# Layer 2 attention: the output step between the third and fourth score, and the maxima at set places

## The reference

```python
qkv = x @ w_qkv
q, k, v = jnp.split(qkv, 3, axis=-1)
q, k, v = (to_heads(q), to_heads(k), to_heads(v))
q = _apply_rope(q, cos, sin)
k = _apply_rope(k, cos, sin)
scores = jnp.einsum('bhqd,bhkd->bhqk', q, k) * scale
causal = jnp.tril(jnp.ones((S, S), dtype=bool))
scores = jnp.where(causal, scores, jnp.finfo(scores.dtype).min)
attn = jax.nn.softmax(scores, axis=-1)
out = jnp.einsum('bhqk,bhkd->bhqd', attn, v)
```

## Time and profile before

| | us |
|---|---|
| median of three executions | 1165.45 |
| lowest and highest | 1164.25, 1167.2 |
| the profiled execution | 1160.65 |
| its span, first to last instruction | 1159.4 |
| TensorE busy in the span | 921.2 (79%) |
| VectorE busy | 846.7 (73%) |
| ScalarE busy | 633.1 (55%) |
| GpSimd busy | 519.9 (45%) |
| layer 2's scores (L1974), first and last | 511.2 to 750.1 |
| layer 2's groups of maxima (L1919), first and last | 477.7 to 719.1 |

### The profile page before, as it was taken

How to read it: one execution, slowest core, us unless ns; L and a number is a source line. 1 busy time by engine, 2 the same in 40 slices (tenths; PEclk the granted TensorE clock), 3 DMA queues, 4 the chain that set the end, 5 groups by cost and what they waited for, 6 DMA issues and landing times. The chain is left out here.

```text
span 1159.4 us, 18534 instructions
## 1 busy us (share of the span) xinstructions
PE 921.2 (79%) x5579; PEld 562.6 (49%) x5579; DVE 846.7 (73%) x1648; ACT 633.1 (55%) x1370; POOL 519.9 (45%) x527
## 2 busy tenths in 40 slices
PE   5978799999667866568888888769999285778992
PEld 3423354444445552222223322258999154766981
DVE  7887999999999367878887887176544658986333
ACT  3487799897243443327766667834543293135432
POOL 2066798899501423301111111225653566326763
PEclk9978899999877988759999999959999587868996
DMA  9000000000000301410011110061110200001113
GB/s 318 1 1 1 1 1 1 1 1 1 1 1 0 146 1 34 131 29 23 22 27 18 30 29 3 2 256 38 45 37 27 76 0 1 1 28 47 52 47 123
DMA packets 28014, 46.29 MB, mean 40 GB/s; under 512 B 8720, under 2 KB 16408, under 8 KB 26896
## 3 DMA queue, kind: packets, MB, share of 16 engines
q1 hardware_dynamic: 22672, 34.66, 9.6%
q0 software_dynamic: 4096, 8.35, 2.5%
q10 hardware_dynamic: 1152, 2.10, 0.5%
HBM read 34.45 MB, written 12.58 MB: 41 GB/s over the span
## 5 line engine op out<-in xcount | busy, mean ns | idle before, releaser
L2106 DVE TENSOR_REDUCE sb_l_mxp<-ps 128x2 f32<-128x1024 f32 (+3 forms) x152 | 171.3, 1163 | 41.0 <-PE ps L1919 39.8
L1048 POOL TENSOR_TENSOR sb_gs<-sb_hs,sb_xp 128x512 f32<-128x512 f32 x128 | 162.4, 1304 | 23.9 <-PE ps L680 19.4
L2049 ACT ACTIVATE sb_l_pT<-ps 128x512 f32<-128x512 f32 (+3 forms) x256 | 111.4, 520 | 76.9 <-PE ps L1974 75.7
L680 PE MATMUL ps<-sb_gs,sb_ident 128*128 128x512 f32 x256 | 132.2, 608 | 0.2
L3058 PE MATMUL ps<-sb_hT,sb_f_shared 128*128 x936 | 118.5, 276 | 1.9 <-ACT sb_hT L3091 1.9
L3058 PEld LDWEIGHTS ps<-sb_hT,sb_f_shared 128*128 128x128 f32 x936 | 110.8, 192 | 3.1 <-issue 2.7
L1974 PE MATMUL ps<-sb_l_qk 51*128 51x512 bf16 (+3 forms) x384 | 88.4, 333 | 18.6 <-ACT sb_l_pT L2049 8.3
L3158 POOL DMA_INDIRECT moe_y<-sb_f_rows,sb_f_rowi x64 | 64.2, 1002 | 52.4 <-DVE sb_f_rows L3130 40.1
L3099 ACT ACTIVATE sb_f_hid<-ps 128x512 f32<-128x512 f32 x78 | 46.6, 597 | 73.9 <-PE ps L3058 73.9
L3069 PE MATMUL ps<-sb_sw_f_out,sb_f_hid 128*128 x624 | 82.7, 276 | 0.7 <-DVE sb_f_hid L3119 0.6
L951 ACT ACTIVATE sb_dA<-sb_dt,sb_negA 128x512 f32<-128x512 f32 x109 | 77.8, 713 | 9.7 <-DVE sb_hs L854 9.0
(11 more groups left out here) (418 smaller groups left out, 2139.6 us busy)
## 6 DMA issues: line engine op xcount, KB each, us to landing
sb_sw_f_in<-w_f_in SPq DMA_DIRECT2D x2, 2048.0 KB, 9.9
sb_sw_f_out<-w_f_out SPq DMA_DIRECT2D x2, 2048.0 KB, 12.7
sb_l_qk<-spill SPq DMA_DIRECT2D x112, 32.0 KB
spill<-sb_l_parts SPq DMA_DIRECT2D x12, 256.0 KB, 3.0
moe_y<-c_f_zero SPq DMA_DIRECT2D x1, 2048.0 KB, 9.2
sb_sw_f_up<-w_f_up SPq DMA_DIRECT2D x1, 2048.0 KB, 12.0
moe_h<-sb_f_rows SPq DMA_DIRECT2D x8, 256.0 KB, 4.4
sb_f_rows<-moe_y SPq DMA_DIRECT2D x8, 256.0 KB, 6.1
```

What stands on the lines that cost most here:

```text
L680: pe.matmul(ps[:, 4 + e * CPB + hf, :], ident[:], gs[:, p % SL, :], start=False, stop=n == DS - 1).then_inc(acc, 1)
L1048: gp.tensor_tensor(gs[:, q % SL, :], hs[:, q % SL, :], cs[:, k % 2, hf * CH:(hf + 1) * CH], ALU.mult).then_inc(times_c, 1)
L2049: ac.activation(pT[e % 3][:, h, 0:width], ps[:, bank[n_bank], 0:width], ACT.Exp, scale=L2_SCALE).then_inc(exped, 1)
L2106: dv.tensor_reduce(dst, src, AX_X, ALU.max).then_inc(max_out, 1)
```

## The change

Two edits in `order()`, and one step is split.

- **Output between scores.** If the output that is pending belongs to a block without a mask, it is issued behind the third score of the next block, not behind the fourth. If it belongs to a masked block it stays behind the fourth. So it moves in B1 to B4. To go with it, the copy moves from behind the second score to behind the first.
- **Set places for groups.** A flag `may` is true only behind an output of a masked block, behind a third score while such an output is pending, behind a fourth score when the output has already been issued, and at the start of a set. Only there may groups be taken, as many as the lead then asks for. In B1 to B4 all groups thus stand behind the fourth score, two at a time.
- **`largest` split from `rows`.** VectorE's reduction to the largest is a step of its own, one group earlier: behind the first group of the next set, before its second ("all").

```diff
@@ -1771,6 +1771,8 @@
                   ("heads", 7, 1, 0, 512, 0), ("heads", 7, 1, 0, 512, 1), ("heads", 7, 2, 512, 384, 0), ("heads", 7, 2, 512, 384, 1),
                   ("diagonals", 0, 7)]
 
+        is_diagonal = lambda qc, kt: kt * P >= qc * CH
+
         def lead(at):
 
             knots = [(0.0, LEAD), (NSET - 2.0, NSET - 2.0 + LEAD), (NSET - 1.25, NSET)]
@@ -1780,16 +1782,18 @@
             return NSET + 1
 
         def order():
-
+            at_gap = lambda step: step[0] == "pv" and is_diagonal(*step[2:4]) or step[0] == "score" and (
+                step[4] == 2 and bool(pending) and is_diagonal(*pending[0][2:4]) or step[4] == 3 and not pending)
 
             out_cost = sum((qc + 1) * CH - max(qc * CH, kt * P) + 100 for qc in range(CPB) for kt in range((qc + 1) * TPC)) * HG
 
             def maxima(s):
                 for i, group in enumerate(GROUPS):
                     yield ("max", s, group), s + (i + 1) / len(GROUPS)
-                    if s > 0 and i == 1:
-                        yield ("rows", s - 1), s + (i + 1) / len(GROUPS)
+                    if s > 0 and i < 2:
+                        yield (("largest", "rows")[i], s - 1), s + (i + 1) / len(GROUPS)
                 if s == NSET - 1:
+                    yield ("largest", s), s + 1
                     yield ("rows", s), s + 1
                 yield None, None
 
@@ -1805,7 +1809,9 @@
                         for h in range(HG):
                             done += width + 100
                             yield ("score", s, qc, kt, h, q0, width), s + done / out_cost
-                            if h == 1 and u > 0 and kt == 1:
+                            if h == 2 and pending and not is_diagonal(*pending[0][2:4]):
+                                yield pending.pop(), s + done / out_cost
+                            if h == 0 and u > 0 and kt == 1:
                                 yield ("copy", u - 1), s + done / out_cost
                             if h == 1 and u > 0 and kt == 2:
                                 yield ("back", u - 1), s + done / out_cost
@@ -1821,9 +1827,10 @@
                         (U // 2 + 1, 5): ("project", 1), (U - 1, 4): ("turn", 2), (U - 1, 6): ("project", 2)}
             pending = []
             at_max, at_out, s_max, s_out = 0.0, 0.0, 0, 0
+            may = True
             gen_max, gen_out = maxima(0), None
             while s_out < NSET:
-                if s_max < NSET and at_max < lead(at_out if gen_out else s_out):
+                if s_max < NSET and may and at_max < lead(at_out if gen_out else s_out):
                     step, at = next(gen_max)
                     if at is None:
                         s_max += 1
@@ -1838,9 +1845,11 @@
                 if at is None:
                     s_out += 1
                     gen_out = None
+                    may = True
                 else:
                     yield step
                     at_out = at
+                    may = at_gap(step)
             yield pending.pop()
             yield ("copy", CPB * NSET - 1)
             yield ("back", CPB * NSET - 1)
@@ -1886,7 +1895,6 @@
                 freed_by[bank[-1]] = (x_new, NCH * 4 + step[1] + 1)
         mixed_at = [CPB * (NSET // B * (c // CPB + 1) - 1) + c % CPB + 1 for c in range(NCH)]
         pv_bank = lambda u: spare_bank if u == U - 2 else 7
-        is_diagonal = lambda qc, kt: kt * P >= qc * CH
         pv_steps = [step for step in steps if step[0] == "pv"]
         masked_at = [sum(is_diagonal(qc, kt) for _, _, qc, kt, _ in pv_steps[:e + 1]) for e in range(len(pv_steps))]
 
@@ -2116,9 +2124,10 @@
                     reduce_group(n_max, s, step[2])
                     n_max += 1
                     max_done[s] = n_max
-                elif kind == "rows":
+                elif kind == "largest":
                     dv.wait_ge(max_out, max_done[s])
                     dv.tensor_reduce(mx[:, z, :], mxp[:, z].rearrange("p k h t -> p (h t) k"), AX_X, ALU.max).then_inc(mx_step, 1)
+                elif kind == "rows":
                     dv.wait_ge(max_mm, n_max + 1)
                     dv.tensor_scalar(mxT[:], ps[0:HG * TPB, n_max % 2 * 2, 0:P], -1.0, None, ALU.mult).then_inc(max_out, 1)
                     n_max += 1
```

## The result

The changed kernel took 1176.01 us (median of 4 runs, 1174.85 to 1180.28), beside 1165.48 us for the kernel before (4 runs): the ratio is 1.0105, 95% interval 1.0079 to 1.013. That is 10.5 us slower, where 10.1 were forecast. Compared a second time it was 1.0079 (1.0046 to 1.0113), 1173.25 against 1164.14 us. The profiled execution took 1174.85 us, with a span of 1173.6 us, and is 14.2 us longer than the profiled one of before.

A forecast was written before the change was run, and what follows sets the result against it. TensorE was taken as the bound, with the path of the maxima to the next first score nearly as long. Terms 9.0 + 1.3 + 0.3 - 0.5 = +10.1 us on 1165.45 gave 1175.5 us, range 1166 to 1182.

The forecast's parts named there:

- the sets with groups: Six sets (0 to 5) that hold the next set's groups of maxima: 1.5 us late each, 9.0 us together.
- the set of 31.3 to 31.8 us: Sign that the forecast is right: the time between first scores of successive sets would be 31.3 to 31.8 us.
- the faster rival: Removed waits pay and the maxima keep up: 1.63 us a set, 9.8 over six sets, giving 1155.7 us; chance 0.12.
- B1 and B3: Second and fourth key blocks, second query half: output waits about 1 us for the copy; diagonal group begins at 8.6 us.
- A1: Second key block of the first query half: the output waits for the copy, costing 0.2 us a set.
- The maxima: VectorE's last reductions begin at 9.6 us, pick-up at 13.5 instead of 11.8; next set's first score 1.4 us late.
- The first score waits for the transfers in every set: Sign that the forecast is right: each set's first score waits for the transfers of its maxima.
- TensorE's own row: Cross-check on TensorE alone: a diagonal group waits for a reduction; 1.2 us a set even if transfers were free.
- Set 6: Last diagonal group late by the output ahead, 1.00 us, plus 0.2 and 0.1 from two blocks: +1.3 us (0.5 to 1.8).
- Set 7: No groups; in four blocks the fourth score waits for the previous block's output, 0.1 us each: +0.3 (0 to 1.2).
- The start: Before the first score, moving the largest up removes VectorE's 0.49 us wait: -0.5 us (0 to -0.7).
- The clock rival: Longer pauses cost TensorE its upper clock once in each of seven sets: up to 1186 us, 1181 with half hidden; chance 0.08.

The follow-up runs named there:

- free places: The change without its set places, so groups of maxima may go wherever the ratio of work asks for one: 1167.7 us, ratio 1.0027.
- e_largest: The kernel before with only the largest moved, behind the first group of maxima: 1161.4 us, ratio 0.9962.
- e_places: The change with every output behind the fourth score of its block, as before, and the set places kept: 1164.0 us, ratio 0.9995.

## Why the prediction was right, and where its terms were off

The sum, +10.1 us, met +10.5 (and +9.1 the second time). The mechanism held, but that the number did is partly luck: the sets with groups were put 2.0 us too high, and a fall of the clock in set 7, left to a rival, gave 1.8 us back. Of the signs named, the set of 31.3 to 31.8 us did not come (30.96); the pick-up did come later than the 12.1 us that would have spoken for the faster rival (13.20). By its own steps:

- *B1 and B3.* The output in B1 waited 1.05 us for the copy (about 1 was forecast), and the diagonal group began 8.47 us behind B1 (8.6). Right.
- *A1.* Forecast 0.2 a set. Its output did wait 0.17 us for the copy (581.68), but from A0 to B1 it took 11.24 us (578.18 to 589.42), and 11.21 before. So this term was nothing.
- *The maxima.* Three reductions and "largest" took 3.75 us to the pick-up, not 3.70 + 0.25 (rows overlap: before, the next instruction started 3.61 us behind the first of the three, 591.82 to 595.43), so the pick-up came 13.20 us behind B1, not 13.5. The casts took 1.64 us instead of 1.97, since the first of them no longer met a select of GpSimd (last section). **This is the mis-sized term**: A0 at 19.72 us instead of 20.3, so +0.8 a set, where I took 1.5. Over stretches 0 to 5 the six sets came to 1.92 + 0.98 + 0.80 + 0.82 + 1.77 + 0.69 (stretch 5 of the second profile, where the mean clocks are equal) = 7.0 us, not 9.0. The 1.92 of stretch 0 is twice a steady set's loss, at a clock of 0.79; no run shows how much of it is order and how much clock.
- *The first score waits for the transfers in every set.* Right in substance, though TensorE's row shows no idle time there: the score starts 0.04 to 0.05 us behind the last landing in the three steady stretches, but, in the set shown, only 0.06 us later than TensorE alone would have allowed. TensorE's own row was right as a path too: B4's diagonal group waits 1.12 us (1.3 forecast). TensorE's row alone was put at B5 14.5 and A0 19.98 us behind B1; they came at 14.19 and 19.72, so the lower limit of 1.2 a set was 0.3 too high as well.
- *Sets 4 and 5* cost more than a steady set (+1.77 in stretch 4), with the turn's bank as a new wait. The sum had not named it.
- *Set 6:* forecast +1.3, measured +1.18, but not all for the stated reason. Stretch 6 is 0.81 us longer, where 1.0 for the output, 0.2 for A1 and 0.1 for B1 were forecast. The first score of set 7 comes 6.89 us behind its pick-up instead of 6.52, and that is a subtraction of VectorE which takes 0.66 us instead of 0.28 while a select of GpSimd runs (735.08, 0.64 us; last section):

```profile
735.19 0.66 DVE L2141 TENSOR_TENSOR sb_l_mxT<-sb_l_mxT,sb_l_mp 32x128 f32<-32x128 f32 x1
```

- *Set 7:* forecast +0.3 (0 to 1.2). From its first score to its last row of scores it took 24.35 us instead of 22.25, +2.1, outside the bounds. The order alone was forecast right: with free places, the same order in set 7 and a clock of 1.00 it took 22.59 us (742.02 to 764.61), +0.34. The other 1.8 us go with the clock, which was 0.57 over 8 us. The clock rival came true here, in one set, and not in the steady sets, which kept 1.00.
- *The start:* forecast -0.5. From the first group of maxima to the first pick-up it took 26.3 us (481.13 to 507.42) instead of 26.9 (477.68 to 504.56), -0.6. Right.

7.0 + 1.2 + 2.1 - 0.6 = 9.7 us, which the two comparisons, 10.5 and 9.1, enclose. The profiled pair differs by 14.2: stretch 5 has 2.7 us more in it by its clock, and the maxima began 3.45 us later (481.13 against 477.68), in code that the change does not touch; 1.6 us came back behind the loop.

The faster rival named the waits that would go, and one part of it was true: two edits of this change, the copy and the largest, bring 6.7 us by themselves. The sum walked through all the parts together and so did not see that the change holds a gain and two losses. As a split of the whole, from the medians: the two small parts -6.7 us, the outputs between scores +10.3, the set places +5.6 on top of that (1173.3 less 1167.7).

Open: what decides in which execution the clock dips in stretches 3 to 7, and how much of the 10.3 us is that. Its steady part is 0.66 us over seven stretches, 4.6 us. Also open is whether the place of "all" carries the last 0.37 us a set, and what the change's places would cost with the outputs behind.

## What to carry to other kernels

A change made of several small moves may hold gains and losses that hide each other: run the parts alone, since here two of four were worth 6.7 us and the whole cost 10. An output that waits for another engine was cheap here behind the last score of a block and dear ahead of it (0.6 us a set), because whatever stands behind it in the same queue (the fourth score, and through it the maxima of the next set) inherits the wait. And when a group is moved earlier, look first at whose buffers it needs: the diagonal group alone made the set 0.47 us longer, and 0.45 us shorter once the pairs ahead of it were spread.

## What the runs showed of the hardware

**A small cast or subtraction on VectorE is held by a select on GpSimd.** The cast of 32 x 128 numbers (L2129, now L2138) takes 0.21 to 0.22 us. Where it starts inside a select of GpSimd, it ends with it. From the kernel with free places:

```profile
574.31 0.63 POOL L2204 TENSOR_SCALAR_AFFINE_SELECT sb_l_raw<-sb_l_raw 128x512 f32<-128x512 f32 x1 [14.42 <-ACT sb_l_raw L2057]
574.43 0.59 DVE L2138 CAST sb_l_mp<-sb_l_mxT 32x128 bf16<-32x128 f32 x1
```

It ends at 575.02, 0.08 us behind the select. In the kernel before it is 0.53 us (596.37 to 596.90, the select ends at 596.83), in e_largest 0.60. In the changed kernel the select is over 0.36 us before the cast starts, and the cast takes 0.22. The subtraction between the casts (L2141) is held too: 0.66 us instead of 0.28, from 735.19 to 735.85, with a select that ends at 735.72. What VectorE reads from PSUM is not: in the changed kernel the reduction of "all" (601.48) takes its usual 1.23 us over a whole select (601.92 to 602.56), and the pick-up in e_places (569.22) its usual 0.28 inside one (568.99 to 569.63). The hold costs up to 0.38 us on the path to the next set, and it moves with the order. The Trainium skill (SBUF — State Buffer, Who interferes with whom) says that VectorE and GpSimd share a pair of ports under an exclusive lock, so that one waits for the other's whole instruction. These rows agree: the wait is for the end of the select, not a slower cast.

**After the same fall, the clock came back early in some executions and late in others.** At the start of this stage TensorE waits 2.60 us for a transfer (477.14 in the kernel before) and then 1.1 us at a time for reductions; the granted clock falls to 0.50 (1.2 GHz) and stays there beyond 510 us, in all 14 profiles. In nine it is back at 1.00 (2.4 GHz) by 516 to 524 us, in five only by 532 to 541, the same kernel among both. The change, first and second profile:

```profile
516.00:524.00 8.00, 7.13 (x48) 1.92 (x45) 5.78 (x6) 4.18 (x13) 1.92 (x3) 0.66 0.37 64
524.00:542.00 18.00, 15.27 (x135) 5.07 (x135) 13.26 (x20) 11.79 (x25) 1.27 (x2) 1.00 0.01 2
```

```profile
516.00:540.00 24.00, 22.51 (x116) 6.15 (x118) 12.33 (x12) 11.84 (x28) 2.55 (x4) 0.50 0.14 27
540.00:544.00 4.00, 4.00 (x29) 1.21 (x25) 1.98 (x3) 2.77 (x5) 0.00 (x0) 0.84 0.00 0
```

Stretch 0 is 6.4 us longer in the second (39.51 against 33.10). What decides between the two is not shown. A single execution of this kernel can therefore not decide anything under some 6 us, while the steady sets mostly agree to some hundredths of one.
